# A one-column exponential of a constant on ScalarE among the projection copies of a fused decoder layer

## The chip, the cores and the metric

One core of a Trainium2 chip runs the whole program. The metric is the device time of one execution in microseconds (us), as the median of a few executions. A profiled execution of the same program gives the trace.

## The reference

The layer is three blocks, each followed by a layer norm: a recurrent mixer (causal depthwise convolution, minGRU, feed-forward with gelu), cross-attention with 16 heads, and a mixture of experts (top 2 of 16, plus a shared expert). There are 64 sequences of 128 positions with 128 features; the context has 120 positions. Cut to what matters here:

```python
x = layernorm(x + mixer(x))                       # rmsnorm, conv, GRU with sigmoid gates, gelu feed-forward

q = (x @ Wq + bq) / sqrt(64); k = ctx @ Wk + bk; v = ctx @ Wv + bv     # 16 heads of 64
scores = einsum('bthd,bshd->bhts', q, k) + causal mask
attn = softmax(scores, axis=-1)                   # exp(scores - max) / sum
x = layernorm(x + einsum('bhts,bshd->bthd', attn, v) @ Wo + bo)

r = sigmoid(x @ gate_w + gate_b); values, experts = top_k(r, 2)
x = layernorm(x + shared_mlp(x) + sum(values / sum(values) * expert_mlp[experts](x)))
```

## The kernel before

The 64 sequences go through in 16 groups of four. A hand-written software pipeline (`pipeline`) calls `body(a, b, c, d, es)` once a step on every engine. In step b (b = 0 to 15) the groups at work are: the mixer of group a = b+1, the attention of group b, the router and the shared expert of group c = b-1, the experts of group d = b-3, and from step 5 on the gathering and the last layer norm of group b-5. Each engine runs its own list in the order in which `body` is written, and semaphores join them. Nothing is reordered.

A step has a front and ten slots (s = 0 to 9).

**The front** makes the attention's 24 projections, numbered 0 to 23: TensorE writes each into a PSUM bank, ScalarE copies the even ones to SBUF and VectorE the odd ones. 0 to 3 are made at the end of the step before. Projections 12 to 19 are queries (`qT`, line 897 on ScalarE, 1207 on VectorE). Number 12 is in bank sE, 14 in t0, 16 in pvb, 18 in t1. Number 17 is written into t0 again, so TensorE waits for ScalarE's copy of 14; number 21 is written into t1 again and waits for ScalarE's copy of 18. TensorE's order there is: projections 12 to 17, the scores of pair 0 (lines 552 and 557, banks sE and sO), a transpose, projections 18 and 19, another transpose, 20, 21, the shared expert's product (line 644), then in slot 1 the scores of pair 1, which wait for all exponentials of pair 0.

**Softmax.** A pair is half the heads of one sequence, in two banks sE and sO. VectorE takes the negated maximum `nm` of a bank (line 1213), ScalarE the exponential with that bias and a row sum (`b_probs`, line 918, four instructions a bank), VectorE the reciprocal of the sum (`ri`, line 1227), and GpSimd multiplies (`pr`, line 1593). TensorE transposes the result in slot s+2. ScalarE's order before the change is: copies 9 to 12, `c_router` (a tanh, line 931), copies 14 and 16, the exponentials of bank sE of pair 0, copy 18, the shared expert's copy, the exponentials of bank sO.

**Function tables.** ScalarE's functions live in table sets. The compiler puts an ACT_TABLE_LOAD ahead of an activation whose function is not in the set that is loaded. The program has 33 of them: one at the start, and in each of the 16 steps one ahead of the first gelu (line 866, slot 9 of the step before) and one ahead of the first exponential (line 918). Copy, identity, square and tanh need none in either set.

**GpSimd** also issues the indirect transfers. In steps 3, 5, 7, ... 15 eight scatters (line 1621) of two finished groups stand between its front work and the first `pr`; from step 5 on four gathers (line 1633) stand there too in every step. When the last of these eight scatters has landed, SyncE loads `xq`, the rows of the experts' first tile, and TensorE transposes them in slot 1 (line 416, m<-xq), ahead of the mixer's product (line 447) and the transposes of pair 0. In the other steps `xq` was loaded in the step before.

Of the kernel before, what the change touches and what calls it, by code (L numbers as in the profile page):

```python
# [18 lines left out]
ACT = mybir.ActivationFunctionType  # L19
# [6 lines left out]
P = 128  # L26
# [73 lines left out]
def layer_kernel(nc, x, ctxT, w_pw, w_gru, w_ff1, w_ff2, cols, rows, w_q, w_k, w_v, w_o, w_e, w_rs, w_sd, out):  # L100
    with ExitStack() as ctx:
        def sb(name, shape, dt=F32):
            return ctx.enter_context(nc.sbuf_tensor(name, shape, dt))
# [3 lines left out]
        def later(g):  # L107

            return not (isinstance(g, int) and g == 0)

        def upto(name, g, k=0):

            return g * PER_GROUP[name] + (k + 1) * (16 if name.endswith(("loaded", "stored")) else 1)

        def whole(name, g):

            return g * PER_GROUP[name] + PER_GROUP[name]
# [5 lines left out]
        def pair(name, shape):  # L123

            return sb(f"{name}_hi", shape, F32R), sb(f"{name}_lo", shape, F32R)
# [14 lines left out]
        eps = sb("eps", [P, SEQ])  # L140
# [12 lines left out]

        cT = sb("cT", [P, SW]); cS = pair("cS", [P, SW])
        vv = sb("vv", [S, SEQ, H * DK]); kT = sb("kT", [P, NCH, SW]); qT = sb("qT", [P, NCH, W])
        nm = sb("nm", [P, 2, 2, 4]); pr = sb("pr", [P, RING, 2, 4, S]); rsum = sb("rsum", [P, 2, 2, 4, 1])
        pT = sb("pT", [S, 8, T]); ri = sb("ri", [P, 2, 2, 4, 1]); hT = sb("hT", [P, NCH, T])
        xa = sb("xa", [P, P]); st2 = sb("st2", [P, 6]); mv2 = sb("mv2", [P, 2]); ve2 = sb("ve2", [P, 1]); rs2 = sb("rs2", [P, 1])
# [94 lines left out]
        def c_(name, n=1):  # L253
            k = COLS.index(name)
            return col[:, k:k + n]
# [536 lines left out]
        def _(act):  # L792
            f = nc.scalar.activation
# [81 lines left out]
            def b_project(b, lo, hi):  # L875
                for n in range(lo, hi):
                    if n % 2:
                        continue
                    act.wait_ge(sem["proj"], upto("proj", b, n))
                    src = proj_banks[n]  # L880
                    kind, j = projections[n]
                    if n == 12 and not later(b):
                        act.wait_ge(sem["w_lo"], len(SPLIT))
                    if n == 0:

                        if later(b):
                            act.wait_ge(sem["scores"], whole("scores", b - 1))
                    if n == 8:

                        if later(b):  # L890
                            act.wait_ge(sem["pv"], whole("pv", b - 1))
                    if kind == "v":
                        ins = f(vv[:, j // 2, (j % 2) * 512:(j % 2) * 512 + 512], src[0:S, :], ACT.Copy)
                    elif kind == "k":
                        ins = f(kT[:, j, :], src[:, 0:SW], ACT.Identity, bias=c_(f"bk{j}"))
                    else:
                        ins = f(qT[:, j, :], src[:], ACT.Identity, bias=c_(f"bq{j}"), scale=DK ** -0.5)
                    ins.then_inc(sem["proj_act"], 1)
# [23 lines left out]
            def c_x2T(c):  # L922
                act.wait_ge(sem["x2T"], upto("x2T", c))

                if later(c):
                    act.wait_ge(sem["rs"], whole("rs", c - 1))
                f(x2T[0][:], m0[:], ACT.Copy).then_inc(sem["x2T_hi"], 1)

            def c_router(c):
                act.wait_ge(sem["logits"], upto("logits", c, 1))  # L930
                f(rt[:], lg[:], ACT.Tanh, scale=0.5).then_inc(sem["route_tanh"], 1)
# [52 lines left out]
            def body(a, b, c, d, es):  # L984
                A, B, C, D = a is not None, b is not None, c is not None, d is not None

                if B:
                    b_project(b, 4, 6)
                if C:
                    c_x2T(c)  # L990
                if A:
                    a_sums(a, 0)
                if B:
                    b_project(b, 6, 8)
                if B:
                    b_project(b, 8, 9)
                    a_x1T(b)
                if C:
                    c_shared(c)
                if B:  # L1000
                    b_project(b, 9, 13)
                if C:
                    c_router(c)
                if B:
                    b_project(b, 13, 18)
                    b_probs(b, 0, 0)
                    b_project(b, 18, 20)
                if C:
                    c_sharedT(c)
                if B:  # L1010
                    b_probs(b, 0, 1)
                if A:
                    a_norm(a, 0)
                for s in range(PAIRS + LAG):
                    if B and s >= LAG:
                        b_probs_T(b, s - LAG)
                    if B and 0 < s < PAIRS:
                        b_probs(b, s, 0)
                    if B and s == 1:
                        b_project(b, 22, 23)  # L1020
                    if B and 0 < s < PAIRS:
                        b_probs(b, s, 1)
                    if B and s == 0:
                        b_project(b, 20, 21)
                    if D and s > 1 and s % 2:
                        d_y(QUADS * d + (s - 3) // 2)
                    if D and s % 2 and s < 9:
                        d_xT(QUADS * d + (s - 1) // 2)
                    if D and s > 1 and s % 2 == 0:
                        d_tanh(QUADS * d + s // 2 - 1)  # L1030
                    if c == G - 1 and s > 1 and s % 2 == 0:
                        w_load(LAST + (0, 1, 6, 7)[s // 2 - 1])
                    if A:
                        if s == 0:
                            a_conv(a)
                        elif s == 2:
                            a_sums(a, 1)
                            if not later(a):
                                w_high(SPLIT[2:5])
                        elif s == 3:  # L1040
                            a_norm(a, 1)
                        elif s == 4:
                            a_gate(a)
                        elif s == 5:
                            a_hid(a)
                        elif s == 7:
                            a_sums(a, 2)
                            if not later(a):
                                w_high(SPLIT[5:])
                        elif s == 8:  # L1050
                            b_project(a, 0, 2)
                            a_norm(a, 2)
                            b_project(a, 2, 4)
                        elif s == 9:
                            for k in range(FCH):
                                a_gelu(a, k)
# [693 lines left out]
```

## Time and profile before

| | us |
|---|---|
| median of 3 runs | 1594.81 (1594.42 to 1595.85) |
| the profiled execution | 1600.01 |
| its span on the core | 1598.3 |
| TensorE busy | 1325.3 (83%) |
| VectorE busy | 1021.7 (64%) |
| ScalarE busy | 877.6 (55%) |
| GpSimd busy | 835.5 (52%) |

The mean granted TensorE clock of the profiled execution is 0.947. The steps take about 85 to 92 us each. No engine is busy all the time: TensorE has the most work, and the rest of a step is a ring of short waits between TensorE, VectorE, ScalarE and GpSimd. The page's chain of work that ended last reaches back only through the tail of the program, so the steps have to be read from timelines.

### The profile page before, as it was taken

The numbers are of one execution on the slowest core, as the hardware profiler recorded it, in microseconds if no ns is written. First come the engines' busy times: TensorE is split into PE (matmuls) and PEld (weight loads), VectorE is DVE, ScalarE is ACT, GpSimd is POOL, SyncE is SP. The second block draws the span as 40 slices with busy tenths as digits, with TensorE's granted clock in tenths as the row PEclk, the third lists the DMA queues.
The fourth block names the chain that finished last, engine by engine and source line by source line (L and its number), as shares of the span: only waits on it lengthen the run. The fifth ranks groups of instructions, "written<-read, shape, count | busy, mean of one in ns | idle before, by whom it ended". The sixth has DMA issues, their size and how long they took to land. (4 is left out here: it accounts for less than half of the span.)

```text
span 1598.3 us, 34208 instructions
## 1 busy us (share of the span) xinstructions
PE 1325.3 (83%) x11168; PEld 1077.9 (67%) x11168; DVE 1021.7 (64%) x2723; ACT 877.6 (55%) x3239; POOL 835.5 (52%) x996
## 2 busy tenths in 40 slices
PE   2889797989898997989888998989889898986650
PEld 1667676777776776767667776767667776865540
DVE  3566657566656777666776767667776767666233
ACT  3656555475655665575665655575665656553120
POOL 4353435553446546663566545664566545564344
PEclk9999998999999999999999999999999999998575
DMA  6000000032112212132122212133122222133651
GB/s 209 8 7 8 7 8 14 12 99 71 38 55 69 83 57 59 47 110 78 36 63 83 84 50 64 45 101 90 33 65 75 82 60 64 36 91 103 178 158 46
DMA packets 142896, 105.78 MB, mean 66 GB/s; under 512 B 12352, under 2 KB 137856, under 8 KB 142720
## 3 DMA queue, kind: packets, MB, share of 16 engines
q1 hardware_dynamic: 132224, 84.71, 18.4%
q0 software_dynamic: 8192, 16.79, 3.7%
q10 hardware_dynamic: 2304, 2.10, 0.5%
q8 instruction: 90, 1.47, 0.4%
q14 instruction: 86, 0.70, 0.2%
HBM read 69.99 MB, written 33.55 MB: 65 GB/s over the span
## 5 line engine op out<-in xcount | busy, mean ns | idle before, releaser
L1593 POOL TENSOR_TENSOR pr<-pr,ri 128x480 f32<-128x480 f32 x256 | 250.8, 993 | 274.1 <-DVE ri L1227 272.2
L918 ACT ACTIVATE pr<-sE,nm 128x120 f32<-128x120 f32 x512 | 178.0, 360 | 249.4 <-DVE nm L1213 249.3
L918 ACT ACTIVATE pr<-sO,nm 128x120 f32<-128x120 f32 x512 | 179.4, 383 | 0.0
L590 PE MATMUL pvb<-pT,vv 120*64 120x128 f32 x2048 | 142.9, 283 | 43.4 <-DVE pT L1223 43.0
L557 PEld LDWEIGHTS sE<-kT,qT 64*128 64x128 f32 x1024 | 126.4, 191 | 55.0 <-issue 55.0
L1633 POOL DMA_INDIRECT gat<-sorted_y,slot x128 | 127.9, 999 | 65.2 <-issue 47.4
L590 PEld LDWEIGHTS pvb<-pT,vv 120*64 120x64 f32 x2048 | 112.2, 139 | 73.1 <-DVE pT L1223 56.7
L1621 POOL DMA_INDIRECT sorted_x<-x,slot x128 | 128.2, 1002 | 48.9 <-issue 34.5
L557 PE MATMUL sE<-kT,qT 64*128 64x120 f32 x1024 | 150.2, 288 | 0.0
L557 PE MATMUL sO<-kT,qT 64*128 64x120 f32 x1024 | 150.2, 288 | 0.0
L416 PE MATMUL t<-ident_f,pr 128*120 128x128 f32 x1024 | 145.3, 288 | 2.4 <-POOL pr L1593 2.0
L599 PE MATMUL pvb<-wo,hT 128*128 128x128 f32 x1024 | 131.9, 283 | 13.8 <-DVE hT L1237 13.8
L1598 POOL TENSOR_TENSOR ve<-mv,eps 128x1 f32<-128x1 f32 x112 | 21.0, 188 | 230.1 <-DVE mv L1249 224.8
L599 PEld LDWEIGHTS pvb<-wo,hT 128*128 128x128 f32 x1024 | 120.7, 194 | 27.2 <-DVE hT L1237 27.2
L416 PEld LDWEIGHTS t<-ident_f,pr 128*120 128x120 f32 x1024 | 125.8, 146 | 10.7 <-issue 6.4
L1227 DVE RECIPROCAL ri<-rsum 128x4 f32<-128x4 f32 x256 | 44.6, 174 | 135.9 <-ACT pr L918 135.5
L906 ACT ACTIVATE pT<-t 120x512 f32<-120x512 f32 x128 | 78.1, 610 | 92.9 <-PE t L416 92.8
L1237 DVE TENSOR_TENSOR hT<-pvb,col 128x512 f32<-128x512 f32 x128 | 87.6, 685 | 63.1 <-PE pvb L590 61.8
L557 PEld LDWEIGHTS sO<-kT,qT 64*128 64x128 f32 x1024 | 126.4, 191 | 0.0
L918 ACT ACTIVATION_READ_ACCUMULATOR pr<-sO,nm 128x1 f32 x512 | 118.1, 231 | 0.0
L1213 DVE TENSOR_REDUCE nm<-sE 128x4 f32<-128x480 f32 x128 | 83.3, 651 | 49.7 <-PE sO L557 48.9
L918 ACT ACTIVATION_READ_ACCUMULATOR pr<-sE,nm 128x1 f32 x512 | 104.0, 203 | 0.0
(333 smaller groups left out, 3533.6 us busy)
## 6 DMA issues: line engine op xcount, KB each, us to landing
wq<-in_w_e SPq DMA_DIRECT2D x224, 128.0 KB
sorted_y<-yq SPq DMA_DIRECT2D x64, 256.0 KB, 2.5
xq<-sorted_x SPq DMA_DIRECT2D x56, 256.0 KB, 2.8
xt<-in_x SPq DMA_DIRECT2D x16, 256.0 KB, 3.0
sorted_x<-yq SPq DMA_DIRECT2D x16, 256.0 KB, 4.1
out_y<-y SPq DMA_DIRECT2D x64, 64.0 KB, 1.6
cT<-in_ctxT SPq DMA_DIRECT2D x16, 240.0 KB, 3.1
sorted_x<-x,slot POOLq DMA_INDIRECT x128
```

Of the source, the lines that this page charges most:

```text
L416: return nc.tensor.transpose(dst, src, ident[0:src.shape[0], 0:src.shape[0]])
L557: ins = mm(score_banks[r][:, i * S:(i + 1) * S], qT[r * DK:(r + 1) * DK, j, q * T:(q + 1) * T], kT[r * DK:(r + 1) * DK, j, q * S:(q + 1) * ...
L590: ins = mm(pvb[r * DK:(r + 1) * DK, (k // 2) * T:(k // 2 + 1) * T], vv[:, q, h * DK:(h + 1) * DK], pT[:, 4 * r + k // 2, :], start=True, s ...
L599: ins = mm(pvb[:, 0:P], hT[:, j, :], wo[:, j, :], start=(j == 0), stop=(j == NCH - 1))
L906: f(pT[:, 4:8, :], seqs(t1[0:S, :]), ACT.Copy).then_inc(sem["probsT1_sb"], 1)
L918: ins = f(pr[:, p % RING, r, i, :], score_banks[r][:, i * S:(i + 1) * S], ACT.Exp, bias=nm[:, p % 2, r, i:i + 1], accum_out=rsum[:, p % 2, ...
L1213: V.tensor_reduce(nm[:, p % 2, r, :], seqs(score_banks[r][:, 0:4 * S]), AX_X, ALU.max, negate=True).then_inc(sem["negmax"], 1)
L1227: V.reciprocal(ri[:, p % 2, r, :, :], rsum[:, p % 2, r, :, :]).then_inc(sem["rinv"], 1)
L1237: V.tensor_tensor(hT[:, 4 * half:4 * half + 4, :], seqs(pvb[:]), c_(f"bv{4 * half}", 4).unsqueeze(2).to_broadcast([P, 4, T]), ALU.add).the ...
L1593: GP.tensor_tensor(pr[:, p % RING, r, :, :], pr[:, p % RING, r, :, :], ri[:, p % 2, r, :, :].to_broadcast([P, 4, S]), ALU.mult).then_inc(s ...
L1621: GP.indirect_dma_start(out=xs[k % 2], out_offset=bass.IndirectOffsetOnAxis(ap=slot[k % 3][:, m, q:q + 1], axis=0), in_=x2[(2 * k + q // S ...
L1633: GP.indirect_dma_start(out=gat[:, q % 2, m, :], out_offset=None, in_=yd[k % 2], in_offset=bass.IndirectOffsetOnAxis(ap=slot[k % 3][:, m, ...
```

## The change

A tile `warm` of one column is added. In `body` on ScalarE, between the copies 9 to 12 and the router's tanh, one exponential of the constant `eps` is taken into it. Nothing reads it.

```diff
         vv = sb("vv", [S, SEQ, H * DK]); kT = sb("kT", [P, NCH, SW]); qT = sb("qT", [P, NCH, W])
+        warm = sb("warm", [P, 1])
...
                 if B:
                     b_project(b, 9, 13)
+                    f(warm[:], eps[:, 0:1], ACT.Exp)
                 if C:
                     c_router(c)
                 if B:
                     b_project(b, 13, 18)
                     b_probs(b, 0, 0)
                     b_project(b, 18, 20)
```

The compiled program still has 33 table loads; the 16 of line 918 now stand ahead of the new instruction (line 1003). All later line numbers move by one or two.

ScalarE in a step from the second on, before. ash is the shared expert, qT<-sE the copy of projection 12, rt the router's tanh; in brackets are the semaphores that the instruction waits for:

```order
L893 ACTIVATE vv<-t 120x512 [waits proj]
L897 ACTIVATE qT<-sE,col 128x512 [waits proj]
L931 ACTIVATE rt<-lg 128x64 [waits logits]
L897 ACTIVATE qT<-t,col 128x512 [waits proj]
L897 ACTIVATE qT<-pvb,col 128x512 [waits proj]
L918 ACT_TABLE_LOAD [waits negmax]
L918 ACTIVATE pr,rsum<-sE,nm 128x120 [waits probsT]
```

The same place in the changed kernel:

```order
L894 ACTIVATE vv<-t 120x512 [waits proj]
L898 ACTIVATE qT<-sE,col 128x512 [waits proj]
L1003 ACT_TABLE_LOAD
L1003 ACTIVATE warm<-eps 128x1
L932 ACTIVATE rt<-lg 128x64 [waits logits]
L898 ACTIVATE qT<-t,col 128x512 [waits proj]
L898 ACTIVATE qT<-pvb,col 128x512 [waits proj]
L919 ACTIVATE pr,rsum<-sE,nm 128x120 [waits negmax,probsT]
```

The load no longer waits for the maximum (negmax); it stands right behind the copy of projection 12, ahead of the router's tanh and the copies of 14 and 16.

In the first step there is no router, and there the load stands ahead of the wait for the maximum even before the change:

```order
L897 ACTIVATE qT<-sE,col 128x512 [waits w_lo,proj]
L897 ACTIVATE qT<-t,col 128x512 [waits proj]
L897 ACTIVATE qT<-pvb,col 128x512 [waits proj]
L918 ACT_TABLE_LOAD
L918 ACTIVATE pr,rsum<-sE,nm 128x120 [waits negmax]
```

and after it:

```order
L898 ACTIVATE qT<-sE,col 128x512 [waits w_lo,proj]
L1003 ACT_TABLE_LOAD
L1003 ACTIVATE warm<-eps 128x1
L898 ACTIVATE qT<-t,col 128x512 [waits proj]
L898 ACTIVATE qT<-pvb,col 128x512 [waits proj]
L919 ACTIVATE pr,rsum<-sE,nm 128x120 [waits negmax]
```

Here too the load moves ahead of two copies. On the other engines no instruction moves.

## Rows read from the trace of the kernel before

**Rows 1.** The page's first part: busy us (share of the span) xinstructions

```profile
PE 1325.3 (83%) x11168; PEld 1077.9 (67%) x11168; DVE 1021.7 (64%) x2723; ACT 877.6 (55%) x3239; POOL 835.5 (52%) x996
```

**Rows 2.** ScalarE's groups by form: the two table loads of a step (busy, mean ns | idle before)

```profile
L866 ACT ACT_TABLE_LOAD x16 | 20.5, 1283 | 0.3
L918 ACT ACT_TABLE_LOAD x16 | 20.5, 1283 | 33.7 <-DVE nm L1213 33.7
```

**Rows 3.** Stretches, busy of PE, PEld, DVE, ACT, POOL, then PEclk, DMA: steps 6, 8, 14

```profile
563.30:586.64 23.34, 23.34 (x160) 19.32 (x159) 14.81 (x43) 11.25 (x25) 11.25 (x14) 1.00 0.26 75
...
767.51:834.41 66.90, 56.33 (x550) 45.60 (x549) 51.27 (x135) 43.00 (x177) 39.82 (x48) 1.00 0.19 53
...
1310.34:1378.78 68.44, 59.22 (x550) 47.87 (x549) 50.95 (x135) 43.02 (x178) 40.29 (x48) 0.95 0.18 52
```

**Rows 4.** Timeline of ScalarE, front of step 6: start, us, what, [idle before <-releaser]

```profile
580.90 0.69 ACT L897 ACTIVATE qT<-sE,col 128x512 f32<-128x512 f32 x1 [0.80 <-PE sE L422]
581.49 0.25 ACT L931 ACTIVATE rt<-lg 128x64 f32<-128x64 f32 x1
582.30 0.69 ACT L897 ACTIVATE qT<-t,col 128x512 f32<-128x512 f32 x1 [0.57 <-PE t L422]
...
586.64 1.28 ACT L918 ACT_TABLE_LOAD   x1 [2.25 <-DVE nm L1213]
587.94 0.36 ACT L918 ACTIVATE pr<-sE,nm 128x120 f32<-128x120 f32 x1
```

**Rows 5.** Timeline of TensorE, the same stretch: projection 17, projection 21, scores of pair 1

```profile
583.50 0.40 PE L420 MATMUL t<-x1T_s_hi,wq_s_hi 128*128 128x512 f32 x1
583.74 0.40 PE L421 MATMUL t<-x1T_s_lo,wq_s_hi 128*128 128x512 f32 x1
...
590.05 0.49 PE L420 MATMUL t<-wv_s_hi,cS_hi 128*120 128x512 f32 x1 [1.09 <-ACT qT L897]
590.38 0.39 PE L421 MATMUL t<-wv_s_lo,cS_hi 128*120 128x512 f32 x1
...
591.96 0.36 PE L552 MATMUL sE<-mask_b,ident_b 128*128 128x480 bf16 x1
```

**Rows 6.** Timeline of ScalarE at the gelu load ahead of step 5

```profile
471.37 1.28 ACT L866 ACT_TABLE_LOAD   x1
472.67 0.69 ACT L866 ACTIVATE hf<-ma,col 128x512 f32<-128x512 f32 x1
```

**Rows 7.** Waits of TensorE: us in total, times, longest us

```profile
PE t L420 <- ACT qT L897: 16.7, 15, 1.5
...
PE m L416 <- DMA xq<-sorted_x: 14.3, 6, 3.7
```

**Rows 8.** Timeline of GpSimd: the first pr of steps 6 and 7

```profile
590.43 0.98 POOL L1593 TENSOR_TENSOR pr<-pr,ri 128x480 f32<-128x480 f32 x1 [2.36 <-DVE ri L1227]
...
689.03 3.82 POOL L1593 TENSOR_TENSOR pr<-pr,ri 128x480 f32<-128x480 f32 x4
```

**Rows 9.** Timeline of TensorE, slot 1 of steps 3, 7 and 9

```profile
329.47 0.66 PE L416 MATMUL m<-ident_f,xq 128*128 128x128 f32 x4 [2.08 <-DMA xq<-sorted_x]
...
687.98 0.66 PE L416 MATMUL m<-ident_f,xq 128*128 128x128 f32 x4 [2.15 <-DMA xq<-sorted_x]
...
868.43 1.03 PE L416 MATMUL m<-ident_f,xq 128*128 128x128 f32 x4 [2.13 <-DMA xq<-sorted_x]
```

**Rows 10.** Timeline of GpSimd: the pr of pair 2 in steps 3, 7 and 9

```profile
336.99 1.93 POOL L1593 TENSOR_TENSOR pr<-pr,ri 128x480 f32<-128x480 f32 x2 [5.62 <-DVE ri L1227]
...
696.03 2.11 POOL L1593 TENSOR_TENSOR pr<-pr,ri 128x480 f32<-128x480 f32 x2 [3.19 <-DVE ri L1227]
...
876.79 2.12 POOL L1593 TENSOR_TENSOR pr<-pr,ri 128x480 f32<-128x480 f32 x2 [3.47 <-DVE ri L1227]
```

**Rows 11.** Timeline of ScalarE, front of the first step

```profile
63.19 1.28 ACT L918 ACT_TABLE_LOAD   x1
65.37 0.36 ACT L918 ACTIVATE pr<-sE,nm 128x120 f32<-128x120 f32 x1 [0.90 <-DVE nm L1213]
```

## Prediction

> **What bounds the kernel now.** I read the page first: TensorE is busy 83% of the span and ScalarE 55% [rows 1], so no engine is simply full, and a removed instruction is worth only what waits for it. The groups of ScalarE come next, because the change moves a table load. A load takes 1.28 us wherever it stands; the 16 gelu loads have 0.3 us of idle time ahead of them in all, while the 16 of line 918 have 33.7 us, which is 2.25 us each in 15 of them, spent on the maximum of VectorE [rows 2, 4]. So ScalarE stands idle, is then released, and only then loads its table: the load is on the path from the maximum to the exponential. Third, a timeline of that place in step 6, as a model. The maximum ends the wait at 586.64, the load runs to 587.92, the first exponential starts at 587.94 [rows 4]. Further down that queue is the copy of projection 18, and TensorE waits 1.09 us for it at 590.05 before it writes projection 21 [rows 5]; 15 steps have such a wait, 16.7 us in all [rows 7]. Up to there TensorE is full: in the 23.34 us of step 6 that end with the load it is busy 23.34 us [rows 3]. What delays TensorE ahead of the load is therefore paid in full, and what ScalarE saves behind it is gained until something else is late.
>
> Fourth, the stretch behind it, on GpSimd and in the waits for DMA. The steps fall in two kinds. In step 6 the first `pr` of GpSimd waits 2.36 us for the reciprocal, thus for ScalarE [rows 8]. In step 7 it starts at 689.03 with no idle time ahead and takes all four products of pairs 0 and 1 in a row, since eight scatters and four gathers stood ahead of it [rows 8]. In those steps TensorE also waits in slot 1 for `xq`, which is loaded once the scatters have landed: 2.08 us in step 3, 2.15 in step 7, 2.13 in step 9; six steps have this wait, 14.3 us in all [rows 7, 9].
>
> **The change, part by part.**
>
> *The load behind the maximum goes.* The exponential could start 1.28 us earlier after the same maximum [rows 2, 4].
>
> *A load and an exponential come in behind the copy of projection 12.* In step 6 that copy ends at 580.90 + 0.69 = 581.59 [rows 4]. A load ahead of gelu starts with no idle time shown and the next instruction starts 0.02 us after it [rows 6], so the load would run from 581.59 to 582.87. The new exponential has one column. No row shows one; the nearest is the tanh of 64 columns with 0.25 us [rows 4], which is the upper end, and zero the lower. I take 0.20. Successors start about 0.1 us before their forerunner ends (the tanh at 581.49, the copy ending at 581.59), so the exponential costs 0.10 of issue, the router's tanh runs from 582.99 to 583.24, and the copy of 14 from 583.14 to 583.83 in place of 582.30 to 582.99 [rows 4]. The router's tanh comes 1.5 us later; VectorE uses it only behind the maxima of pair 0, which are later still, so that costs nothing. The copy of 16 follows at once and is caught up.
>
> *TensorE pays for the later copy of 14.* Projection 17 takes the same bank and started at 583.50 [rows 5]. Now it starts 0.06 us after the copy (the distance in the wait at 590.05), at 583.89: 0.39 us later. After a wait the first matmul takes 0.33 us to the next one, 590.05 to 590.38, where it takes 0.24 in a full queue, 583.50 to 583.74 [rows 5]: 0.10 more. So projection 17, the scores of pair 0 and the maximum come 0.49 us later. The bounds: 0.39 if the new exponential takes no time, 0.54 at its upper end.
>
> *Sum of a step.* The first exponential comes 1.28 - 0.49 = 0.79 us earlier. TensorE's own queue has moved back by 0.49, which the 1.09 us of waiting at projection 21 covers (it needs 0.79 + 0.49 = 1.28, and has 1.09 plus the 0.10 that a filled queue saves and some overlap): I find 0.79 for the scores of pair 1 as well, since they wait for ScalarE's last exponential of pair 0. The cover is nearly used up, so a second load here would gain nothing.
>
> *Where it stays.* In the kind of step 6, `pr`, the convolution, the maxima and the next exponentials all follow from that ring, and `xq` was loaded a step earlier, so 0.79 us go through to the end of the step. These are steps 1, 2, 4, 6, 8, 10, 12, 14, and 15, where the wait for the copy of 18 is the longest one, 1.5 us [rows 7], and no wait for `xq` is among the six. 9 x 0.79 = 7.1 us.
>
> *Where it is lost.* In steps 3, 5, 7, 9, 11, 13 TensorE arrives 0.79 us earlier and waits that much longer for `xq`; the scatters ahead of it don't move. Gain 0.
>
> *Step 0.* Its load starts at 63.19, ends at 64.47, and the maximum comes only at 65.37 [rows 11]: it was hidden. Here the new place is a pure cost, some 0.4 us of the 0.49 (no router's tanh).
>
> *The clock.* TensorE's waits of the six steps grow from 2.1 to 2.9 us. After the 2.13 us of step 9 the four transposes took 1.03 us, after the 2.15 of step 7 0.66 [rows 9], so about this length of idleness the lower clock comes or does not. Its price shows from there to the `pr` of pair 2: 876.79 - 868.43 = 8.36 us at the lower clock against 696.03 - 687.98 = 8.05, 0.3 us; step 3, where GpSimd is not late, has 7.52 and could lose up to 0.8 [rows 9, 10]. Between 0 and 0.3 + 0.3 + 0.8 = 1.4 us for steps 3, 7, 11; I take 0.6.
>
> Total: -7.1 + 0.4 + 0.6 = -6.1 us. The profiled execution, 1600.01 us with a span of 1598.3, would take 1593.9, its span 1592.2; that is 0.38%, and of the median of 1594.81 it makes **1588.8 us**.
>
> **A rule weighed against the rows.** The rows show a load that follows a copy at once and costs 1.28 us with nothing around it [rows 6]. The Trainium skill, ScalarE: Activation LUTs, "What ACT_TABLE_LOAD costs", gives 1283 ns for the load and about 1380 ns of drain, 2.66 us for a switch. The load agrees to the nanosecond; of the drain no row here shows anything. [...]
>
> **The rivals.**
>
> *A drain that only a busy ScalarE pays.* Were a further delay as long as a load, 1.28 us, to stand at the new place and none at the old, the copy of 14 would end at 585.11, projection 17 would start 1.67 us late, and the exponential 1.28 - 1.77 = -0.49 us, that is 0.49 us later than before. Nine steps make 4.4 us, step 0 1.7: +6.1, or 1601 us. It decides against me once the extra delay is over 0.79 us. Against it: the gelu loads [rows 6]. By the figure of the Trainium skill's page (ScalarE: Activation LUTs, "What ACT_TABLE_LOAD costs") it would be slightly more, some 7 us. Chance 4%.
>
> *The lower clock in the long steps.* Of two steps of one kind, 8 took 66.90 us from its load to the next gelu load at full clock, 14 took 68.44 at 0.95 [rows 3]: 1.54 us. New phases may bring this to other steps. Five more eat up the 6.7 us that I have without a clock cost; from seven on, 10.8 against 6.7 us, the kernel is slower by over 0.2%: 1598.9. For it: waits of over 1 us are everywhere in the ring; against: only one of the two steps shown has it [rows 3], and steps may lose it as well. Chance 5%.
>
> *Something later in the step takes it.* If 0.79 us survive in only three or four of the nine steps, because VectorE's or GpSimd's other work comes due at fixed times, the gain is 3 us or less: 1592 to 1595. For it: GpSimd's queue and SyncE's loads tie the steps together. Against: the transfers of these steps start from the same ring. The same holds if the load stays on the path in another form. Chance 24%.
>
> *All 1.28 us in all 15 steps.* If the copy of 14 held nothing up and `xq` moved too: 19.2 us, 1575.6. Against the first speaks the start of projection 17 right behind a full queue [rows 5], against the second the wait for `xq` [rows 9]. Chance 3%. That the load is not moved at all is excluded by the compiled order, shown with the change.
>
> **How the numbers follow.** My case has 64%: 1588.8, by its bounds from 1587.1 (no clock cost, the small exponential free: 0.89 us in nine steps less 0.3) to 1590.0 (0.74 us in nine steps, less 0.45 and the 1.4 of the clock). The range of 1584 to 1595.5 reaches over the third rival's times and a little below my bounds; about 2 in 10 are outside. A measurement of this kernel tells about 0.2%, 3.2 us, from no change: faster is below 1591.6. That takes my case and the last rival, less what jitter of the clock pushes over: 0.68; within 0.2% 0.25; slower 0.07.
>
> **What would show it.** In the profile after: the 16 loads at line 1003 without a wait for VectorE, 1.28 us each, and the exponential some 0.03 to 0.1 us behind the maximum; the copy of 14 0.8 us after its bank is full; a new wait of TensorE for ScalarE at projection 17, some 0.4 us in 16 steps; that at projection 21 gone or below 0.2 us; the six waits for `xq` near 2.9 us, with more lower clock behind them; steps 1, 2, 4 and so on shorter by 0.8 us, the odd ones from 3 to 13 the same. I am wrong if a gap stands around the new load, if the even steps are not shorter, or if the odd ones are.

## The result and the profile after

The changed kernel took 1587.58 us, the median of six executions (1584.96 to 1589.19), where 1588.8 was forecast, beside 1595.47 us for the kernel before (1594.42 to 1601.70). The measured ratio is 0.9942, with a 95% interval of 0.9920 to 0.9964: faster by 0.58%, where 0.38% was forecast. It is not the quotient of the two medians, which is 0.9951. Two more comparisons of the same two kernels, in the experiments below, gave ratios of 0.9973 and 0.9961. By the ratios the three gains are 9.2, 4.3 and 6.4 us, 6.6 in the mean; by the medians they are 7.9, 4.6 and 4.9 us, 5.8 in the mean. The forecast was 6.1 us.

The profiled execution took 1589.19 us with a mean granted clock of 0.948. The page's first line and its busy times, which answer to [rows 1]:

```profile
span 1587.5 us, 34224 instructions
...
PE 1327.4 (84%) x11168; PEld 1077.3 (68%) x11168; DVE 1021.0 (64%) x2723; ACT 876.1 (55%) x3255; POOL 834.0 (53%) x996
```

ScalarE has 16 instructions more, and no engine has a different amount of work. The difference is in the waits. ScalarE's groups by form, as in [rows 2] (busy, mean ns | idle before):

```profile
L867 ACT ACT_TABLE_LOAD x16 | 20.5, 1283 | 0.3
...
L1003 ACT ACT_TABLE_LOAD x16 | 20.5, 1283 | 0.3
L1003 ACT ACTIVATE warm<-eps 128x1 f32<-128x1 f32 x16 | 3.2, 203 | 0.2
```

Both loads of a step still cost 1283 ns. The second one had 33.7 us of idle time ahead of it, and has 0.3 us now. That idle time still exists; the load merely no longer comes after it. The front of step 6 on ScalarE, from its gelu load to the first exponential (start, us, what, [idle before <-releaser]):

```profile
559.74 1.28 ACT L867 ACT_TABLE_LOAD   x1
...
577.34 0.69 ACT L898 ACTIVATE qT<-sE,col 128x512 f32<-128x512 f32 x1 [0.80 <-PE sE L423]
...
578.05 1.28 ACT L1003 ACT_TABLE_LOAD   x1
579.34 0.20 ACT L1003 ACTIVATE warm<-eps 128x1 f32<-128x1 f32 x1
579.45 0.24 ACT L932 ACTIVATE rt<-lg 128x64 f32<-128x64 f32 x1
579.60 0.67 ACT L898 ACTIVATE qT<-t,col 128x512 f32<-128x512 f32 x1
580.17 0.67 ACT L898 ACTIVATE qT<-pvb,col 128x512 f32<-128x512 f32 x1
583.58 0.36 ACT L919 ACTIVATE pr<-sE,nm 128x120 f32<-128x120 f32 x1 [2.73 <-DVE nm L1215]
```

The exponential starts with its maximum: the reduction of bank sE ends at 583.48, the exponential starts at 583.58. Before it was 586.56 and 587.94. The same stretch on TensorE, projections 17 and 21 and the scores of pairs 0 and 1, and below them the wait for `xq` in step 7:

```profile
580.32 0.50 PE L421 MATMUL t<-x1T_s_hi,wq_s_hi 128*128 128x512 f32 x1 [0.21 <-ACT qT L898]
580.66 0.40 PE L422 MATMUL t<-x1T_s_lo,wq_s_hi 128*128 128x512 f32 x1
...
581.13 0.38 PE L553 MATMUL sE<-mask_b,ident_b 128*128 128x480 bf16 x1
...
585.71 0.47 PE L421 MATMUL t<-wv_s_hi,cS_hi 128*120 128x512 f32 x1
...
587.59 0.36 PE L553 MATMUL sE<-mask_b,ident_b 128*128 128x480 bf16 x1
...
683.60 0.95 PE L417 MATMUL m<-ident_f,xq 128*128 128x128 f32 x4 [2.97 <-DMA xq<-sorted_x]
```

Two executions are laid over each other best at an instruction that the change doesn't touch. The gelu load of step 6 is one: it started at 563.30 before [rows 3] and starts at 559.74 now. Times from there, in us:

| step 6, from its gelu load | before | after | difference | forecast |
|---|---|---|---|---|
| projection 17, first matmul | 20.20 | 20.58 | +0.38 | +0.39 |
| scores of pair 0 | 20.91 | 21.39 | +0.48 | +0.49 |
| first exponential | 24.64 | 23.84 | -0.80 | -0.79 |
| projection 21, first matmul | 26.75 | 25.97 | -0.78 | no wait left |
| scores of pair 1 | 28.66 | 27.85 | -0.81 | -0.79 |

TensorE starts 0.38 us later but shows only 0.21 us of idle time. In a full queue matmuls overlap (one of 0.40 us starts 0.24 us after another), so a delay of up to 0.16 us makes no idle time. Whoever counts the bracket alone reads too little. The waits of TensorE, as in [rows 7] (us in total, times, longest us):

```profile
PE m L417 <- DMA xq<-sorted_x: 17.2, 6, 3.0
...
PE t L421 <- ACT qT L898: 3.5, 16, 0.2
```

The wait for ScalarE's copies was 16.7 us in 15 steps at projection 21. Now it is 3.5 us in 16 steps, at projection 17. The six waits for `xq` grew from 14.3 us to 17.2, though one of those before was 1.5 us longer for a reason of its own (step 5).

Whether the 0.8 us stay in the step can be read safely only where the granted clock is the same in both executions. Step 12, from its gelu load to that of step 13, is such a step. The columns are as in [rows 3]; the kernel before:

```profile
1106.34:1196.58 90.24, 79.70 (x708) 64.93 (x707) 66.11 (x177) 54.15 (x203) 51.08 (x61) 1.00 0.20 59
```

The changed kernel:

```profile
1099.78:1189.19 89.41, 79.76 (x708) 64.84 (x707) 66.11 (x177) 54.12 (x203) 51.02 (x61) 1.00 0.20 59
```

Busy times agree to 0.1 us, the clock is 1.00 in both, and the step is 0.83 us shorter. Step 2, with a clock of 0.94 in both, is 0.66 us shorter. Steps 6 and 10 are 0.84 and 0.88 us shorter, although their clock was 1.00 before and is 0.98 now; the other steps with no wait for `xq` differ by -2.24 to +0.16 us, with unlike clocks. Where in a step a lower clock costs time is told in the part on the prediction.

### The profile page after: what moved, and what is told of

Same layout as the page of the kernel before. It is cut to its first block and busy times, and to the rows that moved or that the text cites. A ratio compares the mean times of both kernels' runs of the same rounds, so it can differ in the third digit from the quotient of the medians.

```text
span 1587.5 us, 34224 instructions
## 1 busy us (share of the span) xinstructions
PE 1327.4 (84%) x11168; PEld 1077.3 (68%) x11168; DVE 1021.0 (64%) x2723; ACT 876.1 (55%) x3255; POOL 834.0 (53%) x996
```

## The experiments

Every timed kernel below had the kernel before run beside it on the same chip. Times are medians; the ratios are given as measured and can differ from the quotient of the medians by up to 0.0013. Edits are cut to what matters and shown against the changed kernel, if nothing else is said. A "front" is the time from the first gelu of a step to its first exponential: 23.33 us before, 22.54 in the changed kernel.

**In which steps does the gain lie?** Two kernels split the change by kind of step, so that each half is measured alone.

```diff
                     b_project(b, 9, 13)
+                    if b not in (3, 5, 7, 9, 11, 13):
                         f(warm[:], eps[:, 0:1], ACT.Exp)
```

> The new exponential, and with it the early load, only in steps 0, 1, 2, 4, 6, 8, 10, 12, 14, 15, in which TensorE does not wait for xq. Theory (the 0.79 us a step pass only there): nearly the whole gain of the changed kernel, 7 us, ratio 0.9955. Rival (every step gives alike, 9.2 us over 16 steps): ten sixteenths, 5.8 us, ratio 0.9964. In the trace: the exponential 0.8 us earlier after the gelu load in these steps, unchanged in steps 3, 5, 7, 9, 11, 13.

Measured: 1586.31 us against 1595.99, a ratio of 0.9927 (0.9908 to 0.9947). The front is 22.46 to 22.55 us in the steps that have the early load, and still 23.3 us in the six others. The gain in time is larger than expected: the interval holds neither the theory's 0.9955 nor the rival's 0.9964, and between the medians lie 9.7 us. So the time does not decide between the two, and the steps have to. Steps 1, 2, 4, 6, 8 and 10 are shorter than before by 0.78, 0.80, 0.77, 0.77, 0.78 and 0.79 us, at equal clock in all but step 8 (0.98 here, 1.00 before). Steps 12 and 14 were not alike in clock: +0.16 us with 0.98 beside 1.00, and -2.32 us with 1.00 beside 0.96. Step 10, to be held against the same step before, first before:

```profile
926.21:1017.40 91.19, 79.81 (x707) 64.94 (x706) 67.02 (x176) 54.16 (x202) 51.13 (x61) 1.00 0.20 56
```

and this kernel:

```profile
919.32:1009.72 90.40, 79.89 (x707) 64.84 (x706) 66.88 (x176) 54.02 (x204) 51.11 (x61) 1.00 0.20 57
```

The other half:

```diff
                     b_project(b, 9, 13)
+                    if b in (3, 5, 7, 9, 11, 13):
                         f(warm[:], eps[:, 0:1], ACT.Exp)
```

> The early load only in steps 3, 5, 7, 9, 11, 13, the ones in which TensorE waits for xq. Theory (the wait for xq swallows it): no gain but for the clock, between -1 and +2 us, ratio 1.000; the six waits for xq near 2.9 us in place of 2.1. Rival (every step gives alike): 3.5 us less, ratio 0.9978; the six waits unchanged.

Measured: 1596.56 us, ratio 0.9991 (0.9973 to 1.0009). The fronts of the six steps do shorten, to 22.5 us, and in the time nothing is seen of it. The interval is wide, though, and holds the rival's 0.9978 as well as no change; what decides is the trace. The waits of TensorE in this kernel:

```profile
PE m L417 <- DMA xq<-sorted_x: 18.9, 6, 4.3
```

From the first gelu of the step to the transposes of `xq` it took 32.69, 32.60 and 32.59 us in steps 7, 9 and 11, and in the kernel before 32.74, 32.72 and 32.64. In the changed kernel it is 32.77, 32.62 and 32.65. The arrival of `xq` does not move with the attention's front, and 0.8 us gained ahead of it become 0.8 us of waiting. For the whole step, step 13 tells: in five profiles the lower clock falls in the same two places of it, and it took 90.41 and 90.42 us with the late load (the kernel before and the next experiment), 90.38, 90.51 and 90.37 us with the early one (the changed kernel, this one and the repeat below). So the nine steps without that wait, called ring steps from here on, carry the gain, and the six carry none that shows.

**Is it the load, or the additional instruction?** A tanh of the same column needs no load.

```diff
-                    f(warm[:], eps[:, 0:1], ACT.Exp)
+                    f(warm[:], eps[:, 0:1], ACT.Tanh)
```

> The new instruction takes tanh in place of the exponential, at the same place. Tanh is in the loaded set, so the load stays behind the wait for the maximum. Theory (the moved load is all of the effect): no change, ratio 1.000, the first exponential 2.25 + 1.28 us behind the copy of 16 as before, the copy of 14 not late, since 0.57 us of idle time covers the 0.1 us. Rival (the change of phase or the extra instruction does it): a gain of several us.

Measured: 1596.25 us, ratio 0.9997 (0.9978 to 1.0016). Its groups on ScalarE:

```profile
L919 ACT ACT_TABLE_LOAD x16 | 20.5, 1283 | 33.7 <-DVE nm L1215 33.7
...
L1003 ACT ACTIVATE warm<-eps 128x1 f32<-128x1 f32 x16 | 3.1, 193 | 0.0
```

The load is back behind the maximum with its 33.7 us of idle time, the front is 23.3 us again, and the small instruction alone changes nothing that can be measured. The gain belongs to the position of the load.

**Is the 0.49 us at projection 17 the price of the place?** If so, a load that no copy for a waiting TensorE stands behind should bring all of 1.28 us. The exponential moves behind the copy of 16, the last one ahead of the maximum.

```diff
-                    f(warm[:], eps[:, 0:1], ACT.Exp)
                 if C:
                     c_router(c)
                 if B:
                     b_project(b, 13, 18)
+                    f(warm[:], eps[:, 0:1], ACT.Exp)
                     b_probs(b, 0, 0)
```

> The exponential of the constant stands behind the copies of 14 and 16, directly ahead of the wait for the maximum, where ScalarE was idle for 2.25 us. Theory (the load costs at the first place only by making the copy of 14 late): projection 17 is on time, the maximum too, the first exponential comes 1.28 us earlier in place of 0.79; the scores of pair 1 gain 1.2 to 1.28 us, as TensorE's wait of 1.09 us at projection 21 plus the 0.1 us of a filled queue are used up. Nine steps make 11 us, ratio 0.9932, some 3 to 4 us faster than the changed kernel. Rival (TensorE's queue is the bound as soon as its wait is gone, or the place does not matter): the same time as the changed kernel, ratio 0.994 to 0.9955.

ScalarE in step 6 of this kernel:

```profile
582.20 0.69 ACT L898 ACTIVATE qT<-pvb,col 128x512 f32<-128x512 f32 x1 [0.71 <-PE pvb L423]
582.90 1.28 ACT L1007 ACT_TABLE_LOAD   x1
584.20 0.20 ACT L1007 ACTIVATE warm<-eps 128x1 f32<-128x1 f32 x1
585.15 0.36 ACT L919 ACTIVATE pr<-sE,nm 128x120 f32<-128x120 f32 x1 [0.75 <-DVE nm L1215]
```

The load fits into the idle time with 0.75 us to spare. The front is 22.06 us, 1.27 less than before, and the scores of pair 1 come 1.28 us earlier. Step 10 is 1.32 us shorter than the one before that is shown above, again at full clock:

```profile
922.62:1012.49 89.87, 79.67 (x707) 64.91 (x706) 66.90 (x176) 54.22 (x203) 51.08 (x61) 1.00 0.20 57
```

The waits of TensorE:

```profile
PE m L417 <- DMA xq<-sorted_x: 20.4, 6, 3.7
...
PE t L421 <- ACT qT L898: 0.2, 1, 0.2
```

So the step-by-step account holds for the second place too: the 0.49 us were the price of the place. The ratio is as expected (0.9932): 1585.84 us, ratio 0.9923 (0.9897 to 0.9949). But nine steps of 0.49 us should bring 4.4 us over the changed kernel, and of that the time shows less: beside the kernel before, the median gains 10.1 us here and 9.7 with the early load in the ring steps only. The nine executions run from 1573.92 us at a mean clock of 0.957 to 1592.91 at 0.935; the median clock is 0.942, beside 0.950 of the kernel before in that comparison and 0.951 of the first experiment.

**Repeats, and the place between.** The changed kernel and two more late variants ran together on another chip.

> The changed kernel itself once more, as the partner of the other three on the same chip. Both theories: ratio 0.994, fronts 0.79 us shorter. The runs together give the time at a given mean granted clock.

Measured: the same kernel as in the result, 1591.58 us against 1596.13, ratio 0.9973 (0.9958 to 0.9987), which leaves out the 0.994 that was expected. One of its twelve executions took 4285.84 us and is not in the ratio; without it the median is 1591.50. Why that one took so long is not known. Its waits of TensorE:

```profile
PE m L417 <- DMA xq<-sorted_x: 18.7, 6, 4.5
...
PE t L421 <- ACT qT L898: 3.5, 16, 0.2
```

The wait at projection 17 is the same to the tenth; that for `xq` differs by 1.5 us from the first profile of this same kernel. The mechanism repeats, the total does so only roughly.

```diff
-                    f(warm[:], eps[:, 0:1], ACT.Exp)
                 if C:
                     c_router(c)
                 if B:
-                    b_project(b, 13, 18)
+                    b_project(b, 13, 15)
+                    f(warm[:], eps[:, 0:1], ACT.Exp)
+                    b_project(b, 15, 18)
```

> The exponential of the constant between the copies of 14 and 16. Theory (only the copy of 14 holds TensorE up): the copy of 16 comes 0.5 us late, but its bank is not needed before projection 19, and the maximum is on time, so the front is as with the load behind the copy of 16: the first exponential 1.28 us earlier than in the kernel before, scores of pair 1 too. Rival (any load between the projection copies costs, since they feed TensorE one by one): 0.8 to 1.0 us.

Measured: 1587.36 us, ratio 0.9944 (0.9925 to 0.9962). ScalarE in step 6:

```profile
574.24 0.69 ACT L898 ACTIVATE qT<-t,col 128x512 f32<-128x512 f32 x1 [0.57 <-PE t L423]
574.94 1.28 ACT L1007 ACT_TABLE_LOAD   x1
576.24 0.20 ACT L1007 ACTIVATE warm<-eps 128x1 f32<-128x1 f32 x1
576.35 0.67 ACT L898 ACTIVATE qT<-pvb,col 128x512 f32<-128x512 f32 x1
```

The front is 22.06 us, as in the kernel with the load behind copy 16. The copy of 16 comes late here, and nobody waits for its bank. Of the three copies only that of 14 holds TensorE up, as the prediction said. Beside the changed kernel of the same comparison this is 4.2 us less at the median, where nine fronts of 0.49 us make 4.4; the intervals of the two ratios just touch.

**Does the wait for `xq` cost clock?** Two kernels tried to keep the late place and spare TensorE the longer waits. In the first the six steps stay as before. The edit is against the kernel with the load behind copy 16:

```diff
                     b_project(b, 13, 18)
+                    if b not in (3, 5, 7, 9, 11, 13):
                         f(warm[:], eps[:, 0:1], ACT.Exp)
                     b_probs(b, 0, 0)
```

> The load behind the copy of 16, but only in steps 0, 1, 2, 4, 6, 8, 10, 12, 14, 15. Theory (in the xq steps the shorter front only lengthens TensorE's wait, to 3.3 us, after which the lower clock comes for longer): the gain of 9 x 1.28 = 11.5 us stays and the mean clock is near 0.950 in place of 0.942, median 1583 to 1585, faster than with all steps by 1 to 4 us. Rival (the low clock has nothing to do with these waits): the same clock and time as with all steps, or slower, as the six steps add their part.

Measured: 1587.87 us (7 executions), ratio 0.9947 (0.9928 to 0.9967). The expectation of 1583 to 1585 us with a clock of 0.950 is missed: the clocks are 0.937 to 0.948, no better than with the late load in all steps (0.939 to 0.953 behind copy 14 on the same chip), but for the profiled execution, which took 1603.33 us at a clock of 0.858 and is not read here. In the second, TensorE works on throw-away transposes ahead of the wait for `xq`:

```diff
+                filled = n % 8 == 0 and 0 <= n < 48
+                if filled:
+                    pe.wait_ge(sem["base"], upto("base", c))
+                    for u in range(FILL):
+                        turn(T_bank(n)[:, (u % QUAD) * P:(u % QUAD + 1) * P], ident[:])
```

with `FILL = 22` and the load behind copy 16.

> The load behind the copy of 16 in all steps, and in slot 1 of steps 3, 5, 7, 9, 11, 13 TensorE makes 22 transposes of the identity into the bank that the xq transposes overwrite, ahead of its wait for xq: about 2.9 us of work in place of idleness of 3.3. Theory (the idle wait brings the lower clock): the transposes of xq take 0.66 us in all six steps, the lower clock behind them is gone, the mean clock rises to about 0.950, and the kernel is 2 to 5 us faster than without the filler. Rival (the lower clock comes from the whole load, not from this wait): no change of the clock; if the filler outlasts the wait, a fraction of a us a step is lost.

Measured: 1586.63 us, ratio 0.9946 (0.9925 to 0.9967). The wait shrank:

```profile
PE m L418 <- DMA xq<-sorted_x: 8.1, 6, 2.6
```

The clock behind it came back. These are stretches of 8 us from the transposes of `xq` on (columns as in [rows 3]); step 7 of the kernel with the late load and no filling:

```profile
687.05:695.05 8.00, 8.00 (x64) 7.04 (x66) 2.60 (x4) 1.75 (x5) 4.75 (x5) 0.64 0.60 174
```

and step 13 of the filled one:

```profile
1220.55:1228.55 8.00, 7.02 (x78) 5.91 (x78) 3.38 (x6) 3.14 (x14) 4.76 (x5) 1.00 0.59 173
```

Over steps 3, 5, 7, 9, 11, 13 the clock of this stretch was 1.00, 0.80, 1.00, 0.79, 1.00, 0.80 before; 0.79, 0.83, 0.79, 1.00, 0.79, 0.79 in the changed kernel; 0.79, 0.59, 0.64, 0.79, 0.83, 0.65 with the late load; 1.00, 1.00, 0.79, 1.00, 1.00, 1.00 with the filling. Between 1.00 and 0.64, TensorE goes from 78 matmuls in 7.02 us busy to 64 in 8.00. The levels between which the clock changes are 2.4 and 1.2 GHz.

How the lower clock goes with the wait shows only over many steps, since the same wait has it in one execution and not in the other: the kernel with the tanh waits about as long as the kernel before and has it behind five of its six waits (0.79, 0.79, 0.58, 0.80, 1.00, 0.81), the kernel before behind three. Counted over nine profiles (all but that of 0.858 and those of the third chip below), it stands behind none of the five filled waits of 0.9 to 1.6 us (the sixth, of 2.56 us in step 7, has it), behind 11 of the 17 unfilled waits of 2.0 to 2.7 us, 14 of 16 of 2.7 to 3.2, and 14 of 15 longer ones. So a longer wait for `xq` does go with more lower clock behind it.

But most steps got no shorter: with the filling steps 3, 5, 7, 9, 11 and 13 took 86.95, 88.81, 90.64, 90.26, 90.24 and 90.11 us, without it 87.62, 92.03, 90.10, 89.26, 90.14 and 90.30. Step 3 gained 0.67 us; step 5 gained as well, but varies from profile to profile of the other kernels (90.18 us in the changed one, 91.93 before). GpSimd has 4.75 us of work in that stretch in either case, and I took it that what TensorE does faster waits for it. That is not shown, for in steps 9, 11 and 13 of the filled kernel the lower clock stands in another place, some 70 us after the first gelu, where it costs about 1 us in most steps (below), and this can hide what the filling gave.

The expectation is met in part. The lower clock behind the wait is gone in five of six steps, and the median clock is 0.948 (0.950 expected), beside 0.942 with the load behind copy 14 on the same chip. The time is only 0.7 us below that of the latter, where the filling was to bring 2 to 5.

**The small instruction by itself.** Seven exponentials in place of one, at the change's place and behind copy 16, were to price 0.66 us more of ScalarE's time at each. They ran on a third chip, on which even the kernel before took 1646.81 us. `warm` has seven columns there.

```diff
-                    f(warm[:], eps[:, 0:1], ACT.Exp)
+                    for i in range(7):
+                        f(warm[:, i:i + 1], eps[:, 0:1], ACT.Exp)
```

> Seven exponentials of the constant in place of one, at the place of the change; each further one takes 0.1 us of issue, 0.6 us in all. Theory (the copy of 14 is on TensorE's path, us for us): the first exponential of the softmax comes 0.2 us earlier than in the kernel before in place of 0.79, in all later steps, so 23.1 to 23.2 us after the first gelu. Rival (there is slack between the copy of 14 and projection 17): still 22.55.

One execution with a profile, 1652.37 us. ScalarE in step 8:

```profile
777.74 1.28 ACT L1004 ACT_TABLE_LOAD   x1
779.04 0.76 ACT L1004 ACTIVATE warm<-eps 128x1 f32<-128x1 f32 x7
779.70 0.24 ACT L932 ACTIVATE rt<-lg 128x64 f32<-128x64 f32 x1
```

The seven take 0.66 us from the start of the first at 779.04 to that of the tanh at 779.70, thus 0.09 us each. One of them takes 0.11 (in the changed kernel the tanh starts at 579.45 after 579.34), so six more make 0.55 us. The front of the ring steps is 23.09 us (23.1 to 23.2 expected), and that is 0.55 more than 22.54. At this place whatever ScalarE does for itself goes through to TensorE and comes back in the exponential.

> The same seven exponentials behind the copy of 16. The idle time there, 2.25 us, less 1.28 and 0.1 leaves 0.87, so the further 0.6 fit. Theory: the first exponential of the softmax stays at 22.06 us after the first gelu, 1.28 us earlier than in the kernel before. Rival: 0.6 later.

One execution with a profile, 1644.56 us. ScalarE in step 8:

```profile
774.29 0.76 ACT L1008 ACTIVATE warm<-eps 128x1 f32<-128x1 f32 x7
775.33 0.36 ACT L919 ACTIVATE pr<-sE,nm 128x120 f32<-128x120 f32 x1 [0.28 <-DVE nm L1216]
...
777.56 0.69 ACT L898 ACTIVATE qT<-t,col 128x512 f32<-128x512 f32 x1 [0.76 <-PE t L423]
```

The seven still fit (0.28 us to spare), and the front is 22.06 us in step 4 and 22.14 later: behind the copies 0.55 us more cost at most 0.08. (Of single executions the times, 1652.37 and 1644.56 us, say little beside each other.) But something else appeared from step 6 on: the copy of projection 18 starts 0.76 us late, although its bank was full at 775.7, and the scores of pair 1 come 27.03 us after the first gelu, 0.95 us later than in step 4 of the same execution. Nothing in the trace explains that stall, and it was not pursued.

> The changed kernel a third time, as the partner of the next. By the first two: ratio 0.994 to 0.997.

> The load behind the copy of 14 once more, beside the changed kernel. If the 0.49 us of its front show in nine steps, 4.4 us faster than the changed kernel of this call, ratio to the kernel before 0.991 to 0.9945; if the clock takes it back, the same as the changed kernel.

Measured on that chip: the changed kernel 1641.89 us, ratio 0.9961 (0.9947 to 0.9975); with the load behind copy 14 it is 1638.28 us, ratio 0.9954 (0.9939 to 0.9970). The medians are 3.6 us apart where 4.4 were expected, the ratio is a little above the expected 0.991 to 0.9945, and the intervals of the two overlap widely. The later place was thus ahead in both paired comparisons by nearly what the timeline gives, and no single one of them proves it.

## Why the prediction was right

*The load behind the maximum goes, 1.28 us.* Right. The exponential starts 0.10 us after its maximum. The experiment with a tanh gives the whole of it back, which shows that it is the load's place alone.

*No drain around the load.* Right. In the changed kernel the load ends at 579.33 and the next instruction starts at 579.34, behind copy 16 it is 584.18 and 584.20. The idle time ahead of all 16 loads is 0.3 us in sum. The rival that had a further 1.28 us at a busy ScalarE is out at both places. The 2.66 us for a switch that the Trainium skill gives (ScalarE: Activation LUTs, "What ACT_TABLE_LOAD costs") are contradicted by these rows; its 1283 ns for the load agree with them.

*The small exponential.* I took 0.20 us of duration and 0.10 of issue; 0.203 and 0.11 were measured.

*0.49 us at projection 17.* Right to 0.01 in the table above, and shown by the two kernels that move the load behind the copies of 14 or 16: the front loses another 0.48 us, TensorE's wait for the copies disappears. The form was a little off: I expected some 0.4 us of idle time there and the trace shows 0.21, for the reason told above.

*0.79 us for each of nine steps, 7.1 us.* Right: 0.75 to 0.82 us in the fronts of all steps from 1 to 15, and 0.77 to 0.80 in six whole steps of the kernel that has the early load in the ring steps only. Where a step ran at full clock throughout, the profiles agree closely. Step 8 took 90.24 and 90.22 us with the late load (before, tanh), 89.42 with the early one (the repeat). Step 12 took 90.23, 90.20 and 90.21 us with the late load, 89.41 and 89.39 with the early one; step 14 90.25 and 89.47. What I gave as the third rival, that something later takes the gain, happened in none of these.

*Nothing in the six steps with a wait for `xq`.* Right as far as it can be seen: 0.9991 for these steps alone (with an interval that also reaches to 0.9973), the arrival of `xq` does not move, and step 13 is as long with either load. TensorE's six waits average 2.9 us, as forecast.

*Step 0, +0.4 us.* Not settled. The front of the first step takes 19.13 us before, 19.45 in the changed kernel, but 20.04, 19.69 and 19.68 in the first three experiments, of which the last two load the table there as the kernel before does. The spread of 0.6 us between executions hides the term.

*The clock, +0.6 us.* The direction was right for what I looked at, but the size was too small in step 3, and I had seen only one of two places. In steps 3 to 14 of nine profiles (all but that of 0.858 and those of the third chip) the lower clock stands nowhere but 31 to 42 us after the first gelu, which in the steps with `xq` is the stretch around and behind that wait (in the ring steps it is 37 to 42), and 67 to 76 us after it.

The first place is the one of the forecast. In the changed kernel's profile it came in steps 3, 7 and 11, as forecast, and went from step 9. Step 3 took 86.32 us before, at full clock, and 87.51 to 87.68 us in the seven profiles that have the lower clock there, wherever their load is: 1.2 to 1.4 us, not up to 0.8. In step 7 it is 0.3 to 0.6 us (88.72 without, 89.04 to 89.29 with it), and more where it lasts longer (90.10 with the load behind copy 16). In the ring steps it costs nothing that can be measured: step 6 took 89.80 and 89.77 us with it, 89.87 without.

The second place costs more. Steps 8, 12 and 14 of the kernel with the early load in the ring steps, from first gelu to first gelu (columns as in [rows 3]):

```profile
740.56:830.02 89.46, 81.18 (x707) 66.23 (x706) 66.02 (x176) 54.16 (x204) 51.03 (x61) 0.98 0.20 57
...
1101.08:1191.47 90.39, 81.33 (x707) 66.09 (x706) 65.70 (x176) 54.20 (x204) 51.10 (x61) 0.98 0.20 57
...
1280.93:1370.40 89.47, 79.78 (x707) 64.84 (x706) 66.12 (x176) 54.13 (x203) 51.09 (x61) 1.00 0.20 57
```

And the 8 us of steps 8 and 12 in which the lower clock lies, from 35 and from 68 us after the first gelu:

```profile
775.56:783.56 8.00, 6.31 (x59) 5.14 (x59) 5.91 (x18) 4.61 (x26) 1.97 (x3) 0.79 0.01 2
...
1169.08:1177.08 8.00, 6.55 (x57) 5.36 (x54) 6.23 (x13) 4.44 (x23) 6.13 (x7) 0.79 0.11 33
```

The same step 8 at full clock, in the repeat, took 89.42 us: the lower clock cost 0.04 there. The same step 12 at full clock, in the changed kernel, took 89.41 us: it cost 0.98. When it lasts longer in the second place, as in step 14 of the changed kernel, it costs 1.93 us (91.40 beside 89.47). But step 10 of the changed kernel had it there for nothing (90.31 beside 90.40). TensorE's waits ahead of the second place are the same whether the lower clock comes or not: 1.72 and 1.45 us in the step 12 that has it, 1.71 and 1.44 in the one that hasn't. Why it comes there is open. It falls in other steps in each execution.

In the profiled execution of the changed kernel the steps up to the last gelu are 7.8 us shorter in sum, by terms between -2.24 and +1.19; the rest, from that gelu to the end, is another 3.0 us, though the kernel with the tanh, which gains nothing there, also has it 2.0 us shorter than before. Of the 10.8 us between the two spans nine fronts of 0.79 are 7.1; the other 3.7 lie within what two executions of one kernel differ by.

The total is therefore known to no more than a few us, and that the median came within 1.2 us of the forecast is in part luck. The three measurements of the change, 9.2, 4.3 and 6.4 us by the ratios, lie on both sides of the forecast; the terms of the sum, which can be read inside a step, are known to a few hundredths of a us.

What stays open: why the kernels with the late load have a median clock of 0.942 (0.948 with the filling), where the changed kernel has 0.949 and the kernel before 0.950 and 0.952 (all on the first two chips). The kernel that moves the load behind copy 16 in the ring steps only, which leaves the `xq` waits as before, had 0.942 as well, so those waits are not the whole cause. Their profiles hint where the time went: the longer episodes in the second place, among steps 6 to 14, are two with the load behind copy 16 (steps 6 and 12), two behind copy 14 (10 and 14) and three with the filling (6, 10 and 12), beside two and one in the two profiles of the changed kernel and one before. Each is a single execution, and no run tests it. Open too is the stall in the queue with seven exponentials on the third chip.

## What to carry to other kernels

In this program the table load stood behind what its activation waits for, in every step but the first. Look in the groups for a load with idle time ahead of it: a tiny activation of the same set, put into that idle time, hides the load for 0.2 us of ScalarE. Put it behind the last instruction that another engine waits for, not at the first gap: ahead of the copy that TensorE waited for it gave 0.79 of 1.28 us, behind it all of it. And ask of each step what else arrives late: where a transfer sets the pace, the saved time only becomes a longer wait.

A gain of half a per cent can't be located from two spans. Lay steps of equal granted clock over each other at an instruction that didn't change, and split the change by kind of step. Look also where in the step the clock was lower: the same 8 us at 0.79 cost nothing in one place and 1 us in another.

## What was not expected of the hardware

The time of one kernel moves with its mean granted clock: the kernel before from 1587.69 us at 0.957 to 1603.33 at 0.943, the kernel with the load behind copy 16 from 1573.92 at 0.957 to 1592.91 at 0.935, thus about 1 us for 0.001. These spreads of 16 and 19 us are more than the change is worth. It is no fixed price: the execution at 0.858 took 1603.33 us, only 12 to 19 us more than its six companions at 0.937 to 0.948.

The third chip took 3% longer for the same program (1646.81 against 1596 us). Its steps 5, 7, 9, 11 and 13 took 94 to 97 us in place of 89 to 92, and TensorE's six waits for `xq` are not in its traces (the kernel with the load behind copy 14 has one, of 0.22 us). What the change does in those steps there is not known. There are waits in which an engine waited for nothing that shows, such as this one of TensorE in the kernel with the load behind copy 14:

```profile
PE m L711 <- issue: 10.9, 2, 10.3
```

On that chip times were compared only with one another. What held the engines up is open.
